# Repacking of stacked rows: from a split between ScalarE and VectorE to ScalarE alone, with contiguous reads and stepped writes

## The reference

```
q, k, v = heads(xn @ Wq + bq), heads(xn @ Wk + bk), heads(xn @ Wv + bv)
scores = (q k^T + rel_q + rel_k) / 4            # rel_q[l, r] = q[l] . emb[l - r], rel_k[l, r] = k[r] . emb[l - r]
s = layernorm(softmax(scores) v @ Wo + bo + xn)
y = xn + layernorm(xn) + layernorm(xn) @ mix_w + mix_b
n = layernorm(y)
p = softmax(n @ router_w); combine = the two largest of p in each row, else 0
ffn = y + sum over experts e of combine[:, e] * (silu(n @ w1[e] + b1[e]) @ w2[e] + b2[e])
out = x + s * silu(ffn)
```

## Time and profile before

| | busy us | share of the span |
|---|---|---|
| TensorE matmul (PE) | 1704.5 | 73% |
| TensorE weight load (PEld) | 1233.0 | 53% |
| VectorE (DVE) | 1199.5 | 52% |
| ScalarE (ACT) | 1025.9 | 44% |
| GpSimd (POOL) | 568.0 | 24% |

### The profile page before, as it was taken

How to read it: one execution, slowest core, us unless ns; L and a number is a source line. 1 busy time by engine, 2 the same in 40 slices (tenths; PEclk the granted TensorE clock), 3 DMA queues, 4 the chain that set the end, 5 groups by cost and what they waited for, 6 DMA issues and landing times. The chain is left out here.

```text
span 2322.5 us, 33387 instructions
## 1 busy us (share of the span) xinstructions
PE 1704.5 (73%) x11448; PEld 1233.0 (53%) x11448; DVE 1199.5 (52%) x3110; ACT 1025.9 (44%) x2026; POOL 568.0 (24%) x613
## 2 busy tenths in 40 slices
PE   5638342058888888868888888858888888888884
PEld 2214222047777777757777777734545445445452
DVE  5713657103433333323433333357888787887883
ACT  3425110023333333423333333437776776776762
POOL 2550045611111111111111111101041340432415
PEclk9768665569999889989999999979999999999998
DMA  5443653689998888889998888789888989889871
GB/s 157 127 153 96 199 173 106 209 203 314 310 313 294 277 277 290 288 295 312 308 303 308 282 282 286 269 283 280 246 255 244 272 236 266 257 241 280 254 215 37
DMA packets 469176, 568.87 MB, mean 245 GB/s; under 512 B 60752, under 2 KB 377680, under 8 KB 468624
## 3 DMA queue, kind: packets, MB, share of 16 engines
q1 hardware_dynamic: 425600, 418.70, 56.9%
q0 software_dynamic: 43408, 148.04, 20.5%
HBM read 367.34 MB, written 199.23 MB: 244 GB/s over the span
## 5 line engine op out<-in xcount | busy, mean ns | idle before, releaser
L936 DVE TENSOR_TENSOR rel_out<-rl,rel_tile 128x1024 f32<-128x1024 f32 x256 | 307.8, 1222 | 237.2 <-PE rl L988 170.2
L1181 ACT ACTIVATE scores<-scores,row_least 128x512 f32<-128x512 f32 x512 | 366.3, 717 | 122.4 <-DVE row_least L1216 121.7
L1216 DVE CUSTOM_DVE_ANT_0 scores<-sc,rq 128x512 f32<-128x512 f32 x512 | 338.7, 686 | 90.6 <-issue 88.5
L913 ACT COPY rel_tile<-rl 128x1024 f32<-128x1024 f32 x256 | 249.3, 1017 | 270.4 <-PE rl L988 238.3
L1330 PE MATMUL pt<-ident,scores 128*128 128x128 f32 x2048 | 327.8, 283 | 22.4 <-DVE probsT L1221 14.1
L1009 PE MATMUL up<-rowsT,w 128*128 128x256 f32 x1280 | 330.4, 404 | 3.3 <-DMA w<-in_w 3.3
L1022 PE MATMUL dn<-w,hid 128*128 128x256 f32 x1280 | 321.7, 396 | 0.0
L1330 PEld LDWEIGHTS pt<-ident,scores 128*128 128x128 f32 x2048 | 246.6, 144 | 115.9 <-DVE probsT L1221 75.9
L921 ACT ACTIVATE hid<-up,b 128x256 f32<-128x256 f32 x320 | 134.1, 470 | 389.0 <-PE up L1009 388.3
L1322 PE MATMUL sc<-ks,qs 96*128 96x512 bf16 x512 | 204.1, 399 | 105.7 <-DVE row_least L1216 85.2
L988 PE MATMUL rl<-tabk,krows_sb 96*128 96x128 bf16 x2048 | 157.8, 232 | 150.1 <-DMA krows_sb<-scratch_stack 145.1
(11 more groups left out here) (181 smaller groups left out, 1815.6 us busy)
## 6 DMA issues: line engine op xcount, KB each, us to landing
scratch_rel<-rel_out SPq DMA_DIRECT2D x256, 512.0 KB, 8.6
rq<-scratch_rel SPq DMA_DIRECT2D x512, 256.0 KB, 4.1
w<-in_w POOLq DMA_DIRECT2D x80, 1024.0 KB, 10.9
krows_sb<-scratch_stack SPq DMA_DIRECT2D x768, 64.0 KB, 5.1
scratch_parts<-part SPq DMA_DIRECT2D x96, 128.0 KB
by_head<-scratch_parts SPq DMA_DIRECT2D x16, 768.0 KB
scratch_stack<-by_row SPq DMA_DIRECT2D x4, 3072.0 KB
qrows_sb<-scratch_stack SPq DMA_DIRECT2D x192, 64.0 KB, 8.9
```

What stands on the lines that cost most here:

```text
L913: nc.scalar.copy(both[:, :, u * UN:(u + 1) * UN], rl[r][:].rearrange("p a (b l) -> p l (a b)", l=TILE)).then_inc(s_kc, 1)
L936: nc.vector.tensor_tensor(out[n % SRING][:], rl[r][:].rearrange("p a (b s) -> p (a b) s", s=TILE), both[:, u * UN:(u + 1) * UN], ALU.add). ...
L1181: nc.scalar.activation(sm[j][:, i], sm[j][:, i], ACT.Exp, bias=least[:, j, i:i + 1], scale=-1.0, accum_out=es[:, g % 2, i, j:j + 1]).then_ ...
L1216: nc.vector.tensor_tensor_reduce(sm[j][:, i], sc[i % 2][:], rq[j][:, i], -SM_SCALE, 3.0e38, ALU.add, ALU.min, least[:, j, i:i + 1]).then_i ...
```

## The change

All 16 repacks go to ScalarE. Source and target of the copy are walked in another order: before, for each position its 16 heads (reads 512 bytes apart, writes of 16 neighbours); now, for each head its 256 positions (contiguous reads, writes 256 bytes apart). The number of elements is the same. On ScalarE, (0,3) follows (0,2); (0,4) stands behind `take_v(5)` and ahead of `take_turned(2)`; (0,5) to (0,7) behind `exponents(1)`; (1,0) to (1,2) behind `exponents(2)`; (1,3) to (1,7) behind `exponents(3)`. VectorE's 13 are deleted. The order of the DMAs in SyncE's queue is not touched; with the new shares they wait for ScalarE's count alone.

```
-        ACT_SHARE = (3, 0)
+        ACT_SHARE = (8, 8)
...
         def repacked(half, b):
-            return by_row[:, :, b * H:(b + 1) * H], by_head[b % 2][:].rearrange("k h l -> k l h")
+            return by_row[:, :, b * H:(b + 1) * H].rearrange("k l h -> k h l"), by_head[b % 2][:]
...
             exponents(0)
             repack(0, 2)
+            repack(0, 3)
             take_v(4)
             take_v(5)
+            repack(0, 4)
             take_turned(2)
             take_turned(3)
             exponents(1)
+            repack(0, 5)
+            repack(0, 6)
+            repack(0, 7)
             take_v(6)
             take_v(7)
             take_turned(4)
             take_turned(5)
             exponents(2)
+            repack(1, 0)
+            repack(1, 1)
+            repack(1, 2)
             take_turned(6)
             take_turned(7)
             exponents(3)
+            for b in range(3, B):
+                repack(1, b)
...
-            def repack(half, b):                      # VectorE's, with its 13 calls
-                dve.wait_ge(s_bh[b % 2], 16 * (half * B // 2 + b // 2 + 1))
-                if half:
-                    dve.wait_ge(s_bs, 16 * 2)
-                nc.vector.tensor_copy(*repacked(half, b)).then_inc(s_bd, 1)
```

More of the change, by code:

```diff
@@ L688, in _ @@
             shift(0)
-            repack(0, 3)
-            repack(0, 4)
             normalized(1)
             choose(0)
-            repack(0, 5)
-            repack(0, 6)
-            repack(0, 7)
             residual(4)
@@ L705, in _ @@
             shift(2)
-            repack(1, 0)
-            repack(1, 1)
             normalized(3)
             choose(2)
-            repack(1, 2)
-            repack(1, 3)
             place_pair(2)
             shift(3)
-            repack(1, 4)
-            repack(1, 5)
             choose(3)
             place_pair(3)
-            repack(1, 6)
-            repack(1, 7)
             finish()
```

## The result

The changed kernel takes 2483.19 us in the median (2480.39 to 2491.78, 4 runs), the kernel before 2323.51 (four runs, where 2326.1 is the median of three): a ratio of 1.069, 95% interval 1.065 to 1.073. It is slower by about 160 us, where 2311 us and a range up to 2338 were forecast.

What follows compares the result with a forecast made beforehand. Route was taken as bound by GpSimd, late behind VectorE's repacks, with the layout chain close behind; at 7.1 us a copy the stage ends 15 us sooner, 2324.0 to 2309, or 2311 us on the median; range 2278 to 2338.

Steps and rivals of the forecast that it cites:

- c: Route: time of one ScalarE repack in the new form, taken as 7.1 us; lower end 3.9, upper end 10.3.
- rival B: ScalarE repacks: stepped 2-byte writes cost more than stepped reads; 2338 us at 8.77 a copy, 2362 at 10.3; chance 0.20.
- The slope: ScalarE's chain from 222 us on: each us on the copy time is worth about 16 us above 7.1.
- layout chain: Route's repacks, loads and stores, ending with store_rows(1): predicted to land at 439 to 448 and end the stage last.
- The walk at c = 7.1: Route's new order with 7.1 us a copy: store_rows(1) issued at 414.7, next stage taken at 443, 15 us sooner.
- The end of the block: Route's end: GpSimd's clears to 417.5 plus 13.5 gives 431; after the stores land, 0.6 to 7.5 us more.
- Rivals C and D: Route: overlap gives nothing (gain 2 to 3 us, 2323), or a common end wait decides (within 5 us); chance 0.17 together.
- D: Route's end: something all engines wait for holds the stage, not the order; gain within 5 us; chance 0.17 with the overlap rival.
- The scatter stalls: GpSimd's scatters at line 496, stalled up to 9.83 us beside VectorE's repacks: none above 1.5 us after the move.

Runs made afterwards that it cites:

- e3: The kernel before with 18 forms of copies, 2048 elements on 96 partitions, added at the start of route on ScalarE, then VectorE; only single copy times are read.
- e1: All 16 repacks on ScalarE in the changed kernel's places, but in the old form (stepped reads, neighbouring writes): 2324.73 us, ratio 1.0024 to the kernel before.
- e5: All 16 repacks on ScalarE in the old form, store_back(4) and (5) moved ahead of load(0,7) and store_rows(0): 2298.16 us, ratio 0.9900 to the kernel before.
- e7: All 16 repacks on ScalarE in the old form, GpSimd's 16 clears issued from SyncE's queue ahead of store_rows(1): 2312.42 us, ratio 0.9966 to the kernel before.

## Why the prediction was wrong

*c, the price of one stepped copy: the step that failed.* It was taken as 7.1 us, "a write step costs what a read step does", with 10.3 as the far end. It is 18.7. The row behind it, VectorE's line 628, writes 4 bytes at a time, and for 4 bytes e3 confirms the equality (3.64 and 3.63 us). The match was in part luck: for whole copies e3 puts a 4-byte write step on VectorE at (1.896 - 1.222) / 2048 = 0.3 ns, on ScalarE at (3.637 - 1.897) / 2048 = 0.85. The prediction named the difference ("these writes are of 2 bytes, which no row shows") and bounded it by a factor of two on the step's price, a guess without a row. The step's price on ScalarE is (18.7 - 3.6) / 4096 = 3.7 ns, against 0.9 for a read step, a factor of four. The range should have stayed open on that side, or the chance of rival B been larger.

*The slope was right for the layout chain.* "About 16 us above 7.1" for each us of c, on 18.3 us between starts: 2311 + 16 x 11.2 = 2490; measured 2483. From e1 to the changed kernel `store_rows(1)` goes from 412.3 to 590.0, 177.8 us or 15.9 for each us of c. The next stage starts only 158.8 us later (14.2 for each us), since the end of the block is 19 us shorter: GpSimd's last clear is issued at 536.1, 54 us before the stores, the landing takes 26.8 us from the issue in place of 34.7, and L356 0.2 in place of 11.3. Rival B is the case that came, and its mechanism, ScalarE's layout chain deciding, is what the waits show; its highest price, 10.3, was far too low.

*The walk at c = 7.1 was right up to the issue of the last stores,* within 3 us if one allows for e1's route, which began 1.7 us earlier: pair 0's slots 246.2 (forecast 250.3), store_rows(0) 285.2 (286.4), take_v(6) 319.5 (323), z(3) 356.2 (358.1), pair 2's slots 366.1 (366.8), store_rows(1) 412.3 (414.7). Their landing, 34.7 us, was longer than the 24 to 33 taken.

*The end of the block failed in e1.* It is no part of the changed kernel's loss. The prediction counted 13.5 us behind GpSimd's last issue as a constant and put GpSimd at 431. In e1 its clears share the DMA engines with the 6 MB store and drag to 451, and the block ends at 458.6. Taking the chain's tail as a constant hid that in e1 it was DMA time up to 451, 29 us from the last issue at 421.6. Rivals C and D (a gain of 2 to 3, or within 5 us) come nearest to e1's ratio of 1.0024, and D had the cause in part.

*The scatter stalls* went as forecast: up to 9.83 us beside VectorE's copies of 4.7 us, and no scatter above 1.22 us with all repacks on ScalarE (e1 and the changed kernel). Why a copy on VectorE holds a scatter up, no run shows.

## What to carry to other kernels

In a copy that turns a bf16 layout, try first the step on the read side, with writes that run over neighbours: here, over 16 neighbours, a repack took 7.1 against 18.7 us on ScalarE and 4.7 against 9.4 on VectorE, and in e3 pairs of neighbours 256 bytes apart took 1.91 us on ScalarE against 9.29 for single elements. Before work is moved off a busy engine, see whether those who waited for that engine also wait for a DMA queue: here the move alone won nothing (e1, ratio 1.0024), and with two small stores put ahead of a big one it won 1% (e5, 0.9900). In e1 the last bytes of GpSimd's queue (451), not the big store (landed at 446.9), set the stage's end, so read what still moves between the last issue and the next stage.

## What the runs showed of the hardware

In e3, on ScalarE, 2048 2-byte writes 16 bytes apart take 9.24 us, 4.5 ns each, and 8.74 to 9.29 us at 32, 248 and 256 bytes; 4-byte writes 256 and 16 bytes apart take 3.64 and 3.80 us, 1.8 and 1.9 ns each; two neighbouring 2-byte writes together, then 256 bytes on, take 1.9 ns (1.91 us for 1024 pairs, L563). 2-byte reads 4 bytes apart, with contiguous writes, take 1.897 us (line 543 of e3), as contiguous reads do (1.898). And the tail of GpSimd's DMAs: in e1, 7 us pass between the last byte of its queue (451) and the next stage (458.6); what they are is not settled. In e7, where GpSimd's last scatter was issued at 411.3 and the last stores at 417.8, and in the changed kernel, with its last clear at 536.1 and the stores at 590.0, SyncE's wait at the block's end (L356) is 0.2 us.
